# Attention scores with keys stationary and softmax between VectorE block transposes, in a cross-attention and LoRA-expert kernel

## What is computed

```
q = (layernorm(x) @ Wq + bq)            # 32 heads of 128, in 8 groups of 4
k, v = split(ctx @ Wkv + bkv)           # 8 heads of 128: one for each group
scores = einsum('blkgd,bmkd->bkglm', q, k) / sqrt(128);  attn = softmax(scores, axis=-1)
x = x + (attn @ v) @ Wo + bo                # attn @ v for each head
logits = layernorm(x) @ router_w.T + router_b; gates of the two best of 8 experts
x = x + LoRA experts of rank 16, weighted by the gates
```

## Time and profile before

| | us |
|---|---|
| median of 3 runs | 1196.17 (1193.82 to 1199.01) |
| span of the profiled execution | 1190.4 |
| TensorE busy | 1160.9 (98%) |
| VectorE busy | 641.0 (54%) |
| ScalarE busy | 438.6 (37%) |
| GpSimd busy | 397.7 (33%) |

### The profile page before, as it was taken

The page is one execution under the profiler, slowest core; times in us unless marked ns, Lnnn a source line. Parts: engine busy times, 40 slices in busy tenths (PEclk is TensorE's granted clock), DMA queues, the critical chain, the costliest instruction groups (busy, mean ns, idle before and its releaser), DMA issues.

```text
span 1190.4 us, 16458 instructions
## 1 busy us (share of the span) xinstructions
PE 1160.9 (98%) x6093; PEld 987.3 (83%) x6093; DVE 641.0 (54%) x1084; ACT 438.6 (37%) x730; POOL 397.7 (33%) x323
## 2 busy tenths in 40 slices
PE   7999999799999999999999999999999999999987
PEld 5888888688888888888888888888888888888785
DVE  4454552355555555555555555555555555556966
ACT  3111211443443344334434344444344344433320
POOL 2331451423443244224423342424244324422200
PEclk9999999899999999999999999999999999999988
DMA  8545545220212120202110121112021212121003
GB/s 292 177 124 190 165 124 132 63 80 28 62 27 63 28 62 26 62 26 68 36 54 26 62 62 26 27 61 62 26 71 34 62 26 62 27 46 27 1 2 142
DMA packets 56182, 81.58 MB, mean 69 GB/s; under 512 B 8608, under 2 KB 25032, under 8 KB 56144
## 3 DMA queue, kind: packets, MB, share of 16 engines
q1 hardware_dynamic: 56144, 81.06, 22.9%
HBM read 60.07 MB, written 20.97 MB: 68 GB/s over the span
## 4 chain that ended last, share of the span: by engine, by line
PE 93%; DVE 3%; DMA 2%; ACT 1%; issue 0%; SPq 0%; POOL 0%; DVEq 0%
PE ring L908 25%; PE ring L910 24%; PE ring L909 24%; PE att L1000 5%; PE att L999 5%; PE att L1022 3%; PE att L1023 2%; PE turn L1010 2%; PE turn L921 2%; DMA v_raw<-values_dram 1%; DMA raw<-in_L_xattn_Wkv_dram 1%; DVE pT L631 1%; DVE y L716 1%; PE att L909 0%; PE att L910 0%
## 5 line engine op out<-in xcount | busy, mean ns | idle before, releaser
L908 PE MATMUL ring<-xT_h,w_h 128*128 128x512 f32 x512 | 202.8, 396 | 0.0
L908 PE MATMUL ring<-wo_h,oT_h 128*128 128x512 f32 x512 | 202.2, 395 | 0.0
L910 PE MATMUL ring<-xT_h,w_l 128*128 128x512 f32 x512 | 200.0, 391 | 0.0
L910 PE MATMUL ring<-wo_h,oT_l 128*128 128x512 f32 x512 | 200.0, 391 | 0.0
L909 PE MATMUL ring<-xT_l,w_h 128*128 128x512 f32 x512 | 199.9, 390 | 0.0
L909 PE MATMUL ring<-wo_l,oT_h 128*128 128x512 f32 x512 | 199.4, 389 | 0.0
L720 DVE SCALAR_TENSOR_TENSOR qT_l<-ring,g_bias,qT_h 128x512 fp32r<-128x512 f32 x128 | 96.0, 750 | 171.9 <-ACT qT_h L502 170.9
L716 DVE TENSOR_TENSOR y<-ring,y 128x512 f32<-128x512 f32 x144 | 99.2, 691 | 139.7 <-PE ring L910 139.6
L502 ACT ACTIVATE qT_h<-ring,g_bias 128x512 fp32r<-128x512 f32 x128 | 88.2, 689 | 164.5 <-PE ring L910 164.1
L501 ACT ACTIVATE pT<-turn 64x512 fp32r<-64x512 f32 x128 | 76.0, 594 | 145.5 <-PE turn L1010 143.9
L437 POOL TENSOR_TENSOR s_mem<-s_mem,row_max 128x512 f32<-128x512 f32 x64 | 67.3, 1051 | 180.3 <-DVE row_max L705 180.3
(11 more groups left out here) (118 smaller groups left out, 1986.3 us busy)
## 6 DMA issues: line engine op xcount, KB each, us to landing
v_raw<-values_dram SPq DMA_DIRECT2D x64, 256.0 KB, 3.9
raw<-in_L_xattn_Wkv_dram SPq DMA_DIRECT2D x8, 1024.0 KB, 6.3
values_dram<-s_mem SPq DMA_DIRECT2D x64, 128.0 KB, 2.5
keys_dram<-s_mem SPq DMA_DIRECT2D x32, 256.0 KB, 2.5
raw<-in_L_xattn_Wq_dram SPq DMA_DIRECT2D x8, 1024.0 KB, 5.9
k_raw<-keys_dram SPq DMA_DIRECT2D x32, 256.0 KB, 3.1
raw<-in_L_xattn_Wo_dram SPq DMA_DIRECT2D x8, 1024.0 KB, 5.2
y<-in_ctx_dram SPq DMA_DIRECT2D x16, 256.0 KB, 4.5
```

The lines of the kernel that those rows point to most:

```text
L908: mm(dst, stat[0], mov[0], start=start, stop=False)
L910: return mm(dst, stat[1], mov[0], start=False, stop=stop)
```

## The change

**Scores.** `kT` now holds, for each sequence, high and low keys side by side, and is the stationary operand; the 256 queries (4 heads by 64) are the moving one. A unit's scores are 16 matmuls of 256 columns in place of 32 of 128. They come out transposed: partitions 0 to 63 are the products with the high keys, 64 to 127 those with the low keys.

**Softmax.** ScalarE copies for each half the 64 partitions that are to be added elsewhere (`copy_half`, two copies), VectorE adds in two instructions of 64 partitions (`s_add`) so that the scores of two sequences are stacked on 128 partitions, and transposes 32 by 32 blocks (`transpose` in `s_max`). A row then is split between two neighbouring blocks of 32 partitions, so its maximum and its sum each need an exchange between them: four small ScalarE copies (`swap`), and one more VectorE instruction (`s_peak`; the first in `s_inverse`). After `normalise` VectorE transposes the blocks back (`p_turn`), and the probabilities stand in SBUF (`sT`) as the value product needs them.

**Probabilities and values.** TensorE transposes nothing. `probs_high` and `probs_low` read `sT` in SBUF instead of `turn` in PSUM. The value product writes the banks `turn`, in two halves: one between Q2 and Q3, one between Q3 and O0. Values are split at the end of the unit, after the softmax, on ScalarE and on GpSimd. The own order of unit 1 is gone.

```diff
-                for b in range(UB):
-                    for hp in range(HP):
-                        mm(dst, q_h, kT[:, :, b, :], start=True, stop=False)
-                        last = mm(dst, q_l, kT[:, :, b, :], start=False, stop=True)
+                for b in range(UB):
+                    mm(dst, kT[:, b].rearrange("p i l -> p (i l)"), q_h, start=True, stop=False)
+                    last = mm(dst, kT[:, b].rearrange("p i l -> p (i l)"), q_l, start=False, stop=True)
...
@@ TensorE unit @@
-                queries(g, T, u, 0)
...
-                if not first:
-                    outputs(u)
...
+                for h in range(G - 1):
+                    queries(g, T, u, h)
+                if not first:
...
+                    outputs(u, 0, turn)
+                queries(g, T, u, G - 1)
...
+                    pe.wait_ge(o_low, u * 4 - 2)
+                    outputs(u, 1, turn)
                     out_project(u, out_task(u, 0), out_slot(0), 0)
                 scores(u, first)
...
-                if not first:
-                    turn_probs(u, first)
...
@@ ScalarE @@
+            def swap(dst, src, blocks):
+                for q in (0, 2):
+                    act.copy(dst[q * QR:(q + 1) * QR, blocks], src[(q + 1) * QR:(q + 2) * QR, blocks])
+                    last = act.copy(dst[(q + 1) * QR:(q + 2) * QR, blocks], src[q * QR:(q + 1) * QR, blocks])
...
+                copy_half(u, 0)
+                copy_half(u, 1)
+                swap_max(u, 0)
+                swap_max(u, 1)
+                exponents(u, 0)
+                exponents(u, 1)
+                swap_sum(u, 0)
+                swap_sum(u, 1)
                 act.wait_ge(v_loaded, u * 32 + 32)
                 high(v_h[:], v_raw[:]).then_inc(v_high, 1)
...
@@ VectorE @@
+            def p_turn(u, c):
+                dve.wait_ge(probs_ready, u * 2 + c + 1)
+                nc.vector.transpose(sT[:, cols], low_or_x[:, cols]).then_inc(p_turned, 1)
+            def probs_low(u, c):
+                low(pT[L:P, pairs, 0, :], chunk_of(sT, c)[0:L], pT[0:L, pairs, 0, :])
+                low(pT[0:L, pairs, 1, :], chunk_of(sT, c)[L:P], pT[L:P, pairs, 1, :]).then_inc(p_low, 1)
```

More of the change, by code:

```diff
@@ L459, in unit @@
                 pool.wait_ge(k_high, u + 1)
-                low(kT[:, 1], k_raw[:], kT[:, 0]).then_inc(k_low, 1)
-                pool.wait_ge(v_high, u + 1)
-                low(v_l[:], v_raw[:], v_h[:]).then_inc(v_low, 1)
+                low(kT[:, :, 1, :], k_raw[:], kT[:, :, 0, :]).then_inc(k_low, 1)
+                if T == UNITS - 1 and not last_group:
+                    for c in range(KC):
+                        split_w(step + 1, c)
                 if last_group and T >= 2:
@@ L541, in unit @@
                 last_group = isinstance(g, int) and g == NKV - 1
[L542 to L544 removed]
+                if not first:
+                    probs_high(u, 0)
                 if T == 0:
```

278 lines of the change are left out of this document (151 added, 127 removed).

## The result

The changed kernel takes 1271.32 us (median of 4 runs, 1267.92 to 1275.62); the kernel before takes 1195.7 us beside it. The ratio is 1.063, 95% interval 1.060 to 1.066: 6.3% slower. The profiled execution spans 1266.1 us against 1190.4. Executions of the same kernel differ by up to 0.6% here, so where an experiment has a single run, its effect is read from the loops of its trace and not from its total.

What follows compares the result with a forecast made beforehand. The in-order softmax chain before Q2, no longer TensorE's work, bounds the loop: 29.55 us, 31.0 at T = 1. Units +42.3, start +3.8, end +5.0 and +3: total +54, span 1244.5, with 5.8 for the median 1250 us (1220 to 1272).

Steps and rivals of the forecast that it cites:

- The chain's steps: Softmax times after the first half's last score matmul: copies 1.2, adds 2.6, first maximum 4.05, `p_turn` done 12.95, `query_low` 16.4 us.
- The exchange: Four 32x16 ScalarE copies swapping maxima or sums: 0.65 us, ends 0.45 and 0.85; three on the chain, -0.6 to +0.6.
- The rival of dear transposes: Dear block transposes or exchanges on top of the wait: loop 30.5 to 31.2 us, total 1275 to 1300; chance 0.07.
- The wait behind `v_l`: VectorE's first-half low parts wait for GpSimd's values' split, starting at 15.8 instead of 14.2: +1.6, loop 29.55 us.
- the cheap bound of the earlier trace: A SBUF-to-SBUF sum took 0.63 us beside GpSimd, not held; by it the low parts wait zero, loop 27.95 us.
- T = 1: Units where `wo_l` splits queue behind `v_l`, one getting between the two low parts: 1.3 to 1.5 us more, loop 31.0.
- Start: Unit 0's scores at 214.45, some 11 us idle before unit 1's Q2, clock costing 4.4: +3.8 us at unit 1's scores.
- End: After the last scores: last value product 21.2 us behind them, +5.0, and some +3 for the clock.
- one that falls at the gap before Q2: TensorE's clock drops after idling 3 to 4.4 us there: +31 at T = 1 alone, 1281; all units 1380; chance 0.14.
- its sign, less than 0.95 in the middle: A clock row below 0.95 in the middle of the run would show the clock falling at the gap before Q2.
- The first rival: No wait behind `v_l`: loop 27.95 us, 28.1 with T = 1, total 1193 (1176 to 1212); chance 0.28.
- a hidden chain: If the softmax chain stayed under 14.35 us, TensorE's work alone would set the loop, 25.9 us: total 1131; chance 0.06.

Runs made afterwards that it cites:

- experiment 3: The changed kernel with Q0 read out ahead of the first half's probabilities' high and low parts instead of behind them: 1239.62 us, ratio 1.037 to the kernel before.
- experiment 4: The changed kernel with eight added TensorE transposes of the identity, read by nobody, after O3 of every unit from the second on: 1273.66 us (one run).
- experiment 1: The changed kernel with the values' low parts (`v_l`) replaced on GpSimd by eight fills with zeros, only eight columns still subtracted: 1240.52 us (one run).
- Experiment 2: The changed kernel with the values loaded early and split ahead of the unit's scores, except in unit 0: 1236.69 us, ratio 1.035 to the kernel before.
- experiment 9: The changed kernel with the same work in newly written orders on VectorE, ScalarE and GpSimd: 1166.33 us, ratio 0.976 to the kernel before.
- experiment 7: The changed kernel with the bias copy moved from the start of T = 0 to T = 3 behind `query_low(3)`: 1267.99 us (one run).
- both pairs of kernels: New unit order without and with the tail's own order, 1166.33 and 1169.18 us; both again with bias copy and statistics moved, 1150.64 and 1148.98 us.

## Why the prediction was right

It said 1250 us, slower with 0.70, and gave the mechanism; the runs gave 1271.3, at the upper end of its own forecast of 1220 to 1272. The sum for the span was 1244.5 against 1266.1, 21.6 too low: +24.5 in the 30 units, -3.4 ahead of them, +0.5 behind.

**What bounds it.** Right. TensorE waits before Q2 for VectorE's read-out of Q0, behind the whole chain; experiment 3 frees it by order alone, experiment 4 shows that 1 us more of TensorE's work doesn't count. The scores take 1.91 us, as said (1.84 and a switch).

**The chain's steps** hold up to the first maximum: 1.2, 2.6 and 4.05 were predicted, 1.2, 2.6 and 4.1 measured. **The exchange is the mis-sized term.** Its four copies take 202 ns each as taken, but start every 0.215 us, not overlapped: 0.86 us instead of 0.65. The upper end, 0.85, was the right one; the earlier trace rows had a single such copy, and the overlap was an assumption. Three on the chain are +0.63. The inverse, add and reciprocal with a wait between, takes 0.45 instead of 0.35, another 0.1 to 0.2. `p_turn` starts at 13.1 instead of 12.25, the low parts at 15.1 instead of 14.2; these two terms are 0.7 to 0.8 of the 0.9 us.

**Block transposes**: 0.69 taken, 0.71 and 0.68 measured, 64 each. The 1.24 us, an estimate by the page "VectorE: DVE Perf Modes", section "The three transpose paths", of the Trainium skill, scaled from its 128x128 bf16 figure, would have been too high by 0.5: here the measurement decides, and a transpose of 128x512 in 4-byte elements costs what the maximum (0.69) and the adds (0.68) over 512 elements do. The rival of dear transposes falls.

**The wait behind `v_l`**: right, against the cheap bound of the earlier trace rows. The low parts beside it end 0.5 us after it ends (631.94 + 2.13 = 634.07 against 633.53), as the normalisation in the earlier trace rows did. The Trainium skill, "SBUF — State Buffer", section "Who interferes with whom", said this of instructions with two SBUF inputs, and that a reduction never contends; experiments 1 and 2 and the rows of experiment 9 agree (0.69 us beside `v_l` for the reduction). `v_l` itself ran at 14.3 to 16.7, 0.9 later than in the sum, for the exchanges' sake. With 0.9 for it the predicted 29.55 becomes 30.45; measured 30.17.

**T = 1**: taken at 31.0 (+1.45), measured 32.05 on average (+1.9), but not for the reason given alone. The collision was named and costs 1.0 us, less than taken: the second low part is held to 1.67 us, 0.98 more than alone. The other 0.9 on average is the clock, which falls in four of the seven loops and costs 1.55 us each time. The second pair of low parts is held too (2.55 us instead of 1.39), but no wait of TensorE follows from it.

**Missed**: the bias copy at T = 0. It stands ahead of the low parts, has SBUF on both sides, and the sum didn't count it. It is held in their place, and because ScalarE's `query_high(0)` waits for it, that loop is 30.48 and not 30.17. Seven such loops are 2 us; experiment 7 settles it.

Together: 23 loops at +0.74 are 17.1 us, seven at +1.06 are 7.4, and of these 7.4 the clock is 6.2.

**Start**: 1.57 us of waiting before the first scores (1.4 said), 13.39 us before unit 1's Q2 (11 said). The clock fell there as said, to 0.54 over 225 to 240, but only Q2's matmuls from 233.97 to 238.85 lay in the slow part of that stretch, so it cost 2.4 us and not the 4.4 taken over from the earlier trace rows. The first scores came at 212.93 and not at 214.45, which is nothing to learn from: among the runs that keep this start they lie between 212.9 and 218.6. **End**: +8.5 against +8, with two misses that cancel: the last value product starts 22.96 us behind its scores (+6.7, taken at +5.0), and the rest of the tail, slower clock included, is 1.8 us longer (taken at +3).

**The clock in the middle.** The forecast had a clock that holds, against the rival of one that falls at the gap before Q2. It holds at T = 0, 2 and 3 (1.00 over 570 to 600). At T = 1, where the rival saw its danger, it falls in four loops of seven, at 1.55 us each time and not over a whole unit: 6.2 us, where the rival had 31. So the rival was right in kind and small in size, and its sign, less than 0.95 in the middle, was missed by the page's row of slices, which are too long for it. Half of it was made good by luck, since the collision came out 0.45 us cheaper in each of the seven loops.

**The first rival**, no wait behind `v_l`, had a loop of 27.95. Experiment 2 takes that wait away and has 28.73: the chain as it is without the hold, mis-sized by the same exchanges and inverse. And had it been 27.95, the loop would have stopped at 28.52, where `add_out(3)` behind `p_turn(0)` closes the second cycle, which no sum of the prediction counted. The 1193 of that rival would have been about 1237. The prediction also priced the reward of a hidden chain, 25.9 us a unit, 0.8 below what a unit without waits takes, 26.70.

## What to carry to other kernels

Work taken off the busiest engine brings nothing from the point on at which an in-order chain on the others closes later: add up that chain, step by step with all that is queued ahead of each step, and do it for every read-out the busy engine waits for, not only for the latest. Many tiny instructions are paid by their number: sixteen copies of 512 elements cost the chain 2.3 us a unit here, more than the 0.9 us of the transposes that they helped to remove. Read the clock in windows over single tasks, too: a row of long slices hid four falls that cost 6 us. When such a chain is found, rewrite the lists before giving up the change: the same instructions in another order were 122 us faster.

## What the hardware did that was not expected

- An instruction of 128x4 elements with both sides in SBUF can take as long as what it is held by: 1.71 us for the bias copy and 2.38 us for a statistics operation, both beside `v_l`, against 0.13 to 0.17 alone. Fills on GpSimd, which read nothing, hold the bias copy as well (0.68 us, experiment 1). Who looks only at large tiles misses it. The Trainium skill's section "Who interferes with whom" of "SBUF — State Buffer" names copies and `tensor_scalar` among the instructions that can contend with GpSimd; these two rows agree, at four elements a partition.
- The hold goes both ways: four `wo_l` took 6.79 us beside VectorE's low parts, against 5.41 in the earlier trace rows with one VectorE instruction held in their midst.
- ScalarE's copies of 32x16 do not overlap: 202 ns, one every 0.215 us.
- A block transpose of 128x512 in SBUF is not held by GpSimd, and takes 0.71 us.
- Behind a wait of 2.3 us TensorE's granted clock fell to 1.2 GHz for eight matmuls in four loops of seven, and behind waits of 1.35 and 1.65 us in none.
- In the tail, 3.7 us won in one place came back in another, in both pairs of kernels, for the larger part as time at the lower clock. This was seen, not explained.
